# A wait on GpSimd between pairs of indirect gathers, in a mixture-of-experts, attention, mixture-of-experts kernel

## What is computed

```
x = x + 0.5 * ffn(layernorm(x))
x = x + attn(layernorm(x))
x = x + 0.5 * ffn(layernorm(x))

ffn:   scores = x @ gate_w.T                 # 8 experts
       weights, idx = top_k(softmax(scores), 2), weights / sum(weights)
       y_e = (silu(x @ w1_e.T) * (x @ w3_e.T)) @ w2_e.T     # 512 hidden features
       result = weights[0] * y_idx[0] + weights[1] * y_idx[1]
attn:  each token attends to the 8 earlier tokens of its sequence that are most similar to it
       delta = gelu((mix * x + (1 - mix) * msg) * gain + bias) * scale
```

## Time and profile before

| | |
|---|---|
| runs | 953.4, 954.56, 964.02 us; median 954.56 us |
| span of the profiled execution | 969.8 us; no other time of it is given |
| busy in it | TensorE 738.1, VectorE 577.2, ScalarE 507.0, GpSimd 350.2 us |
| gathers of line 900 | 128, with 64.9 us and 61.6 us of GpSimd's busy time for the two kinds of buffer |
| moved by DMA | 146.45 MB, 151 GB/s in the mean |

### The profile page before, as it was taken

One profiled execution on the slowest core, in us unless ns is written; L12 is line 12 of the kernel. 1 busy time (PEld: TensorE's weight loads), 2 busy tenths in 40 slices (PEclk: granted clock), 3 DMA queues, 4 the chain that ended last, 5 costly groups with the idle time before them and its releaser, 6 DMA issues.

```text
span 969.8 us, 16931 instructions
## 1 busy us (share of the span) xinstructions
PE 738.1 (76%) x4672; PEld 440.1 (45%) x4672; DVE 577.2 (60%) x1652; ACT 507.0 (52%) x948; POOL 350.2 (36%) x378
## 2 busy tenths in 40 slices
PE   3552666997799798759969589989898899928651
PEld 2541234564455465426635345545555545514321
DVE  7388936433477776748958378768765543305424
ACT  6458622632368768448866387856763343303210
POOL 4548750003303361560543245434233000174443
PEclk9765879999799999989989799999999999969776
DMA  9922367665646686676846378778697756747557
GB/s 341 406 70 87 99 154 155 127 130 141 142 91 125 148 163 129 153 171 116 164 114 136 106 130 151 146 141 175 138 187 150 163 120 133 163 118 152 125 132 248
DMA packets 322273, 146.45 MB, mean 151 GB/s; under 512 B 290061, under 2 KB 311181, under 8 KB 321421
## 3 DMA queue, kind: packets, MB, share of 16 engines
q1 hardware_dynamic: 309037, 99.22, 49.8%
q0 software_dynamic: 13152, 46.15, 15.5%
HBM read 33.89 MB, written 41.94 MB: 78 GB/s over the span
## 4 chain that ended last, share of the span: by engine, by line
PE 32%; DVE 14%; issue 14%; SPq 11%; DMA 9%; ACT 8%; another core or an unknown queue 8%; POOL 4%; POOLq 0%; ACTq 0%; DVEq 0%
PE B L1108 18%; PE B L1120 10%; SPq L984 3%; SPq L949 3%; POOL hs L879 3%; DMA t_gh<-t_gp 2%; DVE t_th L1630 2%; DMA t_W<-t_W 1%; PE B L1172 1%; SPq L992 1%; DMA t_ph<-t_p 1%; DVE t_X L1645 1%; DVE t_W L1405 1%; SPq L962 1%
## 5 line engine op out<-in xcount | busy, mean ns | idle before, releaser
L1108 PE MATMUL B<-t_W,t_ht 128*128 x1704 | 410.7, 390 | 68.0 <-issue 29.9
L1108 PEld LDWEIGHTS B<-t_W,t_ht 128*128 128x128 f16 x1704 | 168.6, 100 | 256.9 <-issue 99.3
L1630 DVE SCALAR_TENSOR_TENSOR t_th<-B,t_K,t_th 128x512 f32<-128x512 f32 x142 | 106.0, 747 | 169.0 <-PE B L1108 79.2
L1120 PE MATMUL B<-t_W,t_gh 128*128 x1140 | 151.5, 285 | 52.4 <-ACT t_W L1252 25.6
L1236 ACT ACTIVATE t_th<-B,t_K 128x512 f32<-128x512 f32 x142 | 96.9, 684 | 124.3 <-PE B L1108 55.6
L1120 PEld LDWEIGHTS B<-t_W,t_gh 128*128 128x128 f16 x1140 | 112.6, 102 | 92.6 <-issue 66.5
L900 POOL DMA_INDIRECT t_hp<-ys,t_POSY x64 | 64.9, 1013 | 241.6 <-DMA ys<-t_W 203.5
L879 POOL DMA_INDIRECT hs<-t_s,t_POS x112 | 117.3, 1047 | 75.8 <-DVE t_POS L1533 45.5
L1252 ACT ACTIVATE t_W<-B 128x256 f32<-128x256 f32 x142 | 53.4, 377 | 150.4 <-PE B L1120 76.9
L1636 DVE TENSOR_TENSOR t_gp<-t_th,t_gp 128x512 f16<-128x512 f32 x95 | 66.2, 699 | 64.9 <-ACT t_gp L1245 36.9
L866 POOL TENSOR_TENSOR t_ve<-t_ve,t_mhalf 128x4 f32<-128x4 f32 x24 | 28.1, 1172 | 179.4 <-DVE t_ve L1445 179.3
(11 more groups left out here) (202 smaller groups left out, 906.8 us busy)
## 6 DMA issues: line engine op xcount, KB each, us to landing
ys<-t_W SPq DMA_DIRECT2D x142, 128.0 KB
t_W<-wk POOLq DMA_DIRECT2D x6, 2048.0 KB, 10.9
t_X<-x SPq DMA_DIRECT2D x8, 512.0 KB, 7.6
out<-t_X SPq DMA_DIRECT2D x7, 512.0 KB
hs<-t_ph SPq DMA_DIRECT2D x18, 128.0 KB, 1.9
t_ht<-hs SPq DMA_TRANSPOSE x142
hs<-t_s,t_POS POOLq DMA_INDIRECT x112
t_gh<-t_gp SPq DMA_TRANSPOSE x95
```

The source lines that it names most:

```text
L1108: t = eng.matmul(B[b][:], HT[n % 3][:, (2 * hl + db) * 128:(2 * hl + db) * 128 + 128], W16[:, bass.ds(expert[n] * 4096 + (db * 2048 + wl * ...
L1120: t = eng.matmul(B[b][:, 0:256], GH[n % 3][:, gl, fb * 128:fb * 128 + 128], W16[:, bass.ds(expert[n] * 2048 + (W2OFF + wl * 1024 + fb * 25 ...
L1630: eng.scalar_tensor_tensor(out=th[:], in0=B[b1][:], scalar=K[:, 7:8], in1=th[:], op0=ALU.mult, op1=ALU.mult).then_inc(free[b1], 1)
```

## The change

Each fetch, before its two gathers, waits on GpSimd until both gathers of the fetch before it have landed. `gathered` returns the buffer, the semaphore of its half and the value that the semaphore has when the pair is there; the value was not used on GpSimd before. The first fetch has nothing to wait for, so there are 63 waits. They run across blocks and across layers. Scatters are issued as before. No instruction is moved, and no other engine's program is altered (the line numbers of all code behind shift by four).

```diff
             assert const.n == N_CONST
+            landed = None
             for kind, key in P.order:
...
-                    yg, sem_g, _ = gathered(L, tile)
+                    yg, sem_g, turn = gathered(L, tile)
+                    if landed:
+                        e.wait_ge(*landed)
+                    landed = sem_g, turn
                     for k in range(2):
                         eng.indirect_dma_start(
                             yg[:, k, :], None, ys_d[L][0:128 * last + 128, :],
```

## The result

The change makes the kernel **slower by 6.8%**: 1022.08 us (median of 4, 1016.71 to 1026.46) for 956.27 us of the kernel before (median of 4, 953.4 to 964.02), ratio 1.0677, 95% interval 1.0611 to 1.0742. The forecast was 966 us and its range ended at 994 us. The sign was right and the end became the chain that was expected; the size was wrong, and layer 0, where 14 us were to be gained, gained nothing.

What follows compares the result with a forecast made beforehand. The prediction took TensorE as the bound until the end, where GpSimd's chain of gathers would take over. +25.4 us at the end and -14 us in layer 0 gave +11.4 us, hence 966 us, range 942 to 994 us.

Steps and rivals of the forecast that it cites:

- the chain that was expected: Layer 1's fetches at the end: 32 gather pairs in a row, each awaiting the last landing, make GpSimd the bound.
- the term of a pair: Time from pair to pair in layer 1: 4.8 us beside expert tiles, 4.2 us without, where it was 2.6 us.
- +25.4 us forecast: Layer 1's fetches at the end: 142.2 us from first to last fetch, for 116.85 us before.
- I take half of the 28.9, -14 us: Layer 0's bursts: pauses between gathers give back half of TensorE's 28.9 us of excess idling, a gain of 14 us.
- the 6.6 us of delay for each block: Layer 0: three waits of 2.2 us make each block's last pair land later; a reason for taking only half the gain.
- the standstill: In close bursts of gathers, TensorE's announcements of finished work do not get through, so other engines idle, strongest in layer 1.
- waits between blocks, as predicted: Waits before a block's first fetch cost nothing, since the earlier pair has landed tens of us before.
- `affine` behind the fetches: GpSimd instructions after a block's last pair in layer 0, delayed by the waits and lying on the path to the next block.
- The marker I had set: Sign to check in the new profile: layer 1's first fetch starts 14 us earlier, around 828 us.
- The slower one (984 us): Rival: the pauses give nothing back, the end costs 25.4 us and later `affine` instructions 4 us; chance 0.20.
- The standstill was the real cost: Rival: layer 0 regains some 35 us of idling and lost clock, the end costs 13 us, giving 933 us; chance 0.20.
- The third rival: GpSimd's existing 37.8 us of pauses at the end take in the new waits, layer 0 neutral: 955 us; chance 0.12.

Runs made afterwards that it cites:

- e2: The changed kernel with its waits kept in layer 0 alone, on chip 10: 913.3 us, ratio 1.055 to the kernel before.
- e5: The changed kernel with a wait only before each block's fourth fetch, in layer 0 alone, on chip 14: 879.4 us, ratio 1.019 to the kernel before.
- e6: The changed kernel with a wait only before each block's first fetch, in layer 0 alone, on chip 14: 863.5 us, ratio 0.999 to the kernel before.
- e10: The changed kernel with its waits kept in layer 0 alone, on chip 1: 987.8 us, ratio 1.024 to the kernel before.
- e0_before: The kernel before, without any edit, run and profiled again on chip 10: 860.9 us, ratio 0.997.
- e3: The changed kernel, each fetch waiting for the last pair but one, in both layers, on chip 10: 881.2 us, ratio 1.021 to the kernel before.
- e13: The changed kernel, fetches waiting for the last pair but one, in layer 1 alone, on chip 3: 946.2 us, ratio 0.988 to the kernel before.
- e14: The changed kernel with one `pow` on GpSimd between layer 1's pairs instead of landing waits, on chip 3: 962.0 us, ratio 1.000 to the kernel before.
- e8: The kernel before, without any edit, run and profiled again on chip 1: 976.6 us, where the kernel before has 970.1 us.

## Why the prediction was wrong

**The end, step by step.** That the end becomes a plain chain of pairs was right: GpSimd's waits before line 904 are released by gathers, the chain that ended last runs over gathers from 845 us on, VectorE has no idle stretch of 10 us between 842 us and the last tile, and the 10.5 us behind the last pair stayed (1014.8 - 1003.82 = 11.0). Mis-sized was the term of a pair. The forecast had 4.8 us beside tiles; the 22 steps to 957.80, where TensorE computes its last tile, take 5.22 us in the mean. It had 4.2 us without tiles; the nine steps behind take 5.11 us, seven of them 4.41 to 4.94 and two 7.43 and 6.18. Beside those two SyncE stores outputs (967.46 and 997.99); no run shows whether that is the reason. I had priced a wait by when a join starts, 2.53 us after the gather's end, and had taken the shortest of three such rows. GpSimd itself starts 0.23 to 0.74 us after the join. The value of the other two rows, 3.38 and 3.68 us, would have given 5.6 to 5.9 us; the mean of all three and the 2.26 us, 5.46 us. (The row of the 3.68 us says `issue` and not a gather, so it bounds a landing rather than measures one.) For the +25.4 us forecast, +43.9 came.

**The step that failed is layer 0's**, "I take half of the 28.9, -14 us". It counted what the pauses might give back, and the 6.6 us of delay for each block stood only as a reason to take half. Eight blocks of 6.6 us are 53 us, a term that the sum left out. The chips without the standstill show it bare: 50 us in the runs (e2), 2.1 us for each wait inside a block (e5), nothing for waits between blocks, as predicted (e6). Nor does the carrier look like the one I named: the rows show the joins on VectorE, which stand ahead of expert tiles, rather than `affine` behind the fetches. With the standstill the same waits cost 18 us by the medians and 23 by the ratio (e10), where -14 was forecast. If they cost 50 us there too, the pauses gave back some 30, more than the 14 I had taken; this is a difference between chips and not a measurement. That they gave back something is seen in the same traces: the idle time that ends with `remote` in stage 0 falls from 91.7 to 19.3 us in the first comparison, and from 68.2 to 27.8 on chip 1. The marker I had set, a first fetch of layer 1 fourteen us earlier, failed: TensorE is idle in stage 0 for 86.9 us before and 88.8 after. Its idling only moved from the bursts to the joins.

**Sum.** +43.9 us and, by e10, +18 to +23 for -14: that is 62 to 67 us, for the 66 us of the runs. The 56 us that the forecast lacked are some 32 to 37 us of layer 0 and 18.5 us of the end. The range had a fault of its own: landings of 1.8 to 3.7 us give +10 to +47 us at the end, and with a gain of 5 to 25 us these terms reach from 940 to 997 us, not from 948 to 990. The 1022 us lie outside either, because no end of the range had a loss in layer 0.

**The rivals.** The slower one (984 us) came nearest, but not by its mechanism: the pauses do thin the standstill, and this is not the profiler's, since the unprofiled runs of before differ between chips by 100 us as well. "The standstill was the real cost" has a true half: the kernel before takes about 100 us longer on chips with it, and the changed kernel only 29 us (993.2 and 1022.1 us), with 612.7 and 159.4 us in its stages on chip 14 and 621.4 and 160.8 us in the first comparison. It lost because waiting for each landing costs 131 us by itself, more than those 100. The third rival, pauses that absorb the waits, failed: no pause of 10 us for joins or stores is left at the end of the changed kernel, and e0_before, without the standstill, has none either.

The Trainium skill's advice in "DMA: Bandwidth & Descriptors", section "Rules for kernel authors", to issue early and wait late, agrees with e3, where a wait one pair later costs 18 us instead of 131. The Trainium skill's rule that a DMA engine takes turns between queues (same page, "Queues, rings and completion order") says nothing that would make a burst hold up engines on three chips and not on two others; no run here shows what does.

**What stays open.** What in a chip makes the standstill, and how much of the 100 us between chips is its doing. That spacing removes it and a limit of two pairs does not rests on single traces (e13 and e14, both chip 3). One `pow` of 1.1 us for each pair of gathers costs as much as it gives; a shorter pause was not run.

## What to carry to other kernels

A wait put ahead of an issue can be paid by whoever stands in order behind the data: count it once for each wait inside a burst (2.1 us each here, in layer 0), follow it through the in-order engines that consume the data, and enter it as a term, not as a shade of another. If transfers must be limited, let the wait lag: without the standstill two pairs under way cost 2% and one pair 15%, with it two pairs gain about 1% and one pair costs 7%. Before betting on a stall with an unknown releaser, have the kernel profiled on a second chip; this one ran at 863 or at 956 to 970 us. And look at what takes the stall's place: in e14 the stall is gone and the time is the same.

## What the runs showed of the hardware

On chips 1, 3 and 13 and in the first comparison, consumers of TensorE's results stand still while GpSimd issues indirect DMAs closely, for 16 to 24 us in the worst cases (the earlier trace rows and e8), and idle times there end with a releaser that the profile calls remote; on chips 10 and 14 none ends so, and the same program takes about 100 us less. With pairs of gathers 3.6 us apart instead of 2.5 the end of layer 1 has no such idle time (e14 and e13, chip 3). GpSimd's two small `pow` instructions take 2.13 us, nearly as long as the issue of a pair of gathers (2.26 us), and slow this kernel nearly as much as waiting for the pair to land (71 us for 78 us). TensorE's same matmuls in stage 0 take 514 us at a granted clock of 0.99 (e0) and 530 us at 0.95 (e2), where TensorE idles 43 us more.
